# Inverse of the gated delta rule: X and its transpose on different partition halves, products over four quarters of the TensorE array, Z and X in two PSUM banks

## What is computed

```python
mem = DECAY * mem + sdt
hard = (mem > THR).astype(x.dtype)
...
alpha = jax.nn.sigmoid(abt + alpha_spike * spike)
beta = jax.nn.sigmoid(bbt[..., None] + jnp.sum(spike * beta_spike, axis=-1, keepdims=True))
active = (jnp.sum(hard, axis=-1, keepdims=True) > 0)
alpha = jnp.where(active > 0, alpha, jnp.ones_like(alpha))
beta = beta * active
s = s * alpha[..., None]
u = jnp.einsum('bhd,bhdv->bhv', kt, s)
s = s - beta[..., None] * jnp.einsum('bhd,bhv->bhdv', kt, u)
s = s + beta[..., None] * jnp.einsum('bhd,bhv->bhdv', kt, vt)
out = jnp.einsum('bhdv,bhd->bhv', s, qt)
```

## Time and profile before

| | us |
|---|---|
| median of the 3 timed runs | 1183.43 |
| lowest and highest of them | 1169.3, 1190.45 |
| the profiled execution | 1186.2 |
| its span | 1184.5 |
| PE busy, PEld busy | 1079.8, 769.0 |
| DVE busy, ACT busy | 701.1, 519.5 |

### The profile page before, as it was taken

One profiled execution on the slowest core, in us unless ns is written; L12 is line 12 of the kernel. 1 busy time (PEld: TensorE's weight loads), 2 busy tenths in 40 slices (PEclk: granted clock), 3 DMA queues, 4 the chain that ended last, 5 costly groups with the idle time before them and its releaser, 6 DMA issues. The chain is left out here.

```text
span 1184.5 us, 41088 instructions
## 1 busy us (share of the span) xinstructions
PE 1079.8 (91%) x17266; PEld 769.0 (65%) x17266; DVE 701.1 (59%) x2517; ACT 519.5 (44%) x1500; POOL 200.7 (17%) x390
## 2 busy tenths in 40 slices
PE   7878789999999999999999997898999999899987
PEld 3332278888888888888888884456456456545642
DVE  2887868888878888887776551244336225323610
ACT  7566213444444444444444343144254245325411
POOL 7100101122122122212211201211103001110200
PEclk8999759999999999999999898899999999899999
DMA  2000000000000000000000003100000000000000
GB/s 89 1 1 1 1 2 3 5 4 4 4 4 4 4 5 4 4 4 4 4 27 4 4 4 101 31 1 1 0 9 10 1 9 1 10 1 1 10 1 9
DMA packets 12805, 11.38 MB, mean 10 GB/s; under 512 B 1563, under 2 KB 11407, under 8 KB 12623
## 3 DMA queue, kind: packets, MB, share of 16 engines
q1 hardware_dynamic: 12623, 8.75, 2.5%
HBM read 7.70 MB, written 1.05 MB: 7 GB/s over the span
## 5 line engine op out<-in xcount | busy, mean ns | idle before, releaser
L1220 ACT COPY work<-banks 128x128 f32<-128x128 f32 x160 | 42.8, 268 | 168.8 <-PE banks L926 168.8
L892 PE MATMUL banks<-work 64*64 64x64 f32 x3072 | 102.6, 232 | 6.7 <-DVE gates L599 5.8
L926 PE MATMUL banks<-work,gates 64*64 64x32 f32 x2560 | 105.3, 221 | 3.1 <-issue 2.8
L946 PE MATMUL banks<-work 64*64 64x32 f32 x2560 | 105.5, 223 | 0.4 <-ACT work L1220 0.4
L203 DVE SCALAR_TENSOR_TENSOR mom<-gates 128x16 f32<-128x16 f32 x512 | 101.3, 198 | 5.8
L926 PEld LDWEIGHTS banks<-work,gates 64*64 64x64 f32 x2560 | 93.5, 139 | 15.4 <-issue 11.4
L599 DVE COPY_PREDICATED gates<-work,banks 128x256 f32<-128x256 uint32 x192 | 101.9, 531 | 1.1
L199 DVE SCALAR_TENSOR_TENSOR gates<-mom,gates 128x16 f32<-128x16 f32 x512 | 96.7, 189 | 9.6 <-ACT gates L1193 4.5
L604 DVE TENSOR_TENSOR work<-work,banks 128x128 f32<-128x128 f32 x128 | 36.8, 288 | 101.1 <-PE banks L936 99.9
L936 PEld LDWEIGHTS banks<-work 64*64 64x64 f32 x2048 | 74.2, 139 | 32.9 <-issue 22.3
L946 PEld LDWEIGHTS banks<-work 64*64 64x64 f32 x2560 | 92.2, 139 | 0.5 <-ACT work L1220 0.5
(11 more groups left out here) (235 smaller groups left out, 2348.9 us busy)
## 6 DMA issues: line engine op xcount, KB each, us to landing
qT<-in_x_dram SPq DMA_DIRECT2D x4, 256.0 KB, 4.3
work<-in_x_dram SPq DMA_DIRECT2D x4, 256.0 KB, 4.0
out_dram<-work SPq DMA_DIRECT2D x4, 256.0 KB, 3.1
gates<-in_w_ff_dram SPq DMA_DIRECT2D x3, 256.0 KB, 3.1
wv_sb<-in_wv_dram SPq DMA_DIRECT2D x1, 512.0 KB, 4.9
work<-in_w_out_dram SPq DMA_DIRECT2D x1, 512.0 KB, 5.3
gates<-in_x_Wq_dram SPq DMA_DIRECT2D x1, 512.0 KB, 5.9
gates<-in_x_Wk_dram SPq DMA_DIRECT2D x1, 512.0 KB, 6.6
```

Source lines behind the costliest of these rows:

```text
L892: last = pe.matmul(level_out(l)[to, a], KS[rows, n.two, hp], late[rows, hp], start=True, stop=True)
L926: last = pe.matmul(packed(psZX, l)[rows, hp], EA[rows, n.three, l, hp], first_half(X, l)[rows, hp], start=True, stop=True)
L946: last = pe.matmul(packed(psXT, l)[rows, hp], Z[rows, l - 1, hp], second_half(XT[:, n.two], l)[rows, hp], start=True, stop=True)
L1220: ac.copy(first_half(Z[:, l - 1], l), packed(psZX, l)).then_inc(z_ok, 1)
```

## The change

Slots and halves of the heads are dealt anew, so that `make_z`, `make_x`, `turn_start` and `solve` go round four quarters (`by_time`), with the outputs of the two input halves in different banks: `psZX` is now banks 6 and 7. `make_xt` (`straight`) and `read_chunk` (`halves`) stay on two quarters. XT's output moves to the second half of bank 5, where the spike counts were; the counts go to unused columns of bank 0 (for gates above number 4), by a matmul of their own, `spike_counts`. Orders and waits follow from the shared banks: `spike_sums` moves from the end of l = 3 to between `make_x` and `make_xt` of l = 4, `spike_counts` stands behind that `make_xt`, `drive` moves forward in l = 4, `alpha` moves behind `keep(aft2, 0)`. `start_xt` (ACT) is three copies in place of one. `level` and `make_xt` get waits on the gates.

```diff
-        psZX, psXT = bank[6], bank[7]
+        psZX = paired(6)
+        psZX_half = psZX[:, :, 0:W]
+        psXT = psG[:, B * C:B * C + HP * W].rearrange("p (a n) -> p a n", a=HP)
...
+        def counts(g):
+            if g.n <= HP:
+                return psG[:, B * C:2 * B * C]
+            return psL[:, 0:2, 2 * C:4 * C]
...
+        by_time = [(par, 2 * t + (t + swap) % 2) for par in range(2) for swap in range(2) for t in range(2)]
+        by_parity = [(par, 2 * t + (par + swap) % 2) for t in range(2) for swap in range(2) for par in range(2)]
+        halves = [(par, 2 * t + s) for par in range(2) for s in range(2) for t in range(2)]
+        straight = [(par, 2 * t + s) for par in range(2) for t in range(2) for s in range(2)]
...
+        def at_level(par, hp):
+            return head_rows[hp // 2], 2 * par + (hp // 2 + hp) % 2
+
+        def at_x(par, hp):
+            return head_rows[hp // 2], 2 * (hp % 2) + par
+
+        def at_z(par, hp):
+            return head_rows[hp % 2], 2 * (hp // 2) + par
+
+        def at_xt(par, hp):
+            return head_rows[hp % 2], 2 * ((hp // 2 + hp) % 2) + par
...
                 def alpha(g):
                     ve.wait_ge(al0_ok, g.n + 1)
+                    ve.wait_ge(count_mm, g.n + 1)
...
+                        if l == 4 and gate:
+                            drive(gate)
                         spike(scan, h + 2)
                         if aft:
                             prefix(aft, l)
...
-                        if l == 4 and gate:
-                            drive(gate)
...
                         update(cur, 1)
-                    if gate:
-                        alpha(gate)
...
                         keep(aft2, 0)
+                    if gate:
+                        alpha(gate)
...
-                def level(n, l):
+                def level(n, l, gate=None, gate_old=None):
+                    if l == 1 and gate_old:
+                        pe.wait_ge(alpha_ok, gate_old.n + 1)
+                    if l == 3 and gate_old:
+                        pe.wait_ge(beta_ok, gate_old.n + 1)
...
-                    for hp in range(HP):
-                        for rows in head_rows:
-                            last = pe.matmul(packed(psZX, l)[rows, hp], XT[rows, n.two, hp],
-                                             first_half(Z[:, l - 1], l)[rows, hp], start=True, stop=True)
+                    for head in by_time:
+                        (rows, a), (_, z), (to, q) = at_xt(*head), at_z(*head), at_x(*head)
+                        last = pe.matmul(packed(psZX_half, l)[to, q], XT[rows, n.two, a],
+                                         first_half(Z[:, l - 1], l)[rows, z], start=True, stop=True)
...
-                def make_xt(n, l):
+                def make_xt(n, l, gate, gate_old):
+                    if l == 1 and gate_old:
+                        pe.wait_ge(be0_ok, gate_old.n + 1)
+                    if l == 5 and gate:
+                        pe.wait_ge(zal_ok, gate.n + 1)
...
+                def spike_counts(g, aft=None):
+                    if aft:
+                        pe.wait_ge(e_ok, aft.it * LEVELS + 4)
+                    if g.n:
+                        pe.wait_ge(beta_ok, g.n)
+                    pe.wait_ge(spk_ok, g.n + 1)
+                    pe.matmul(counts(g), bdones[:, :], counts_as(g, spk[:, g.two]), start=True, stop=True).then_inc(count_mm, 1)
...
-                    pe.matmul(psG[:, B * C:2 * B * C], bdones[:, :], spk[:, g.two], start=True, stop=True)\
...
                             make_x(nxt, l)
+                        if l == 4 and gate and gate.n <= HP:
+                            spike_counts(gate)
+                        if l == 4 and gate:
+                            spike_sums(gate)
                         if nxt:
-                            make_xt(nxt, l)
+                            make_xt(nxt, l, gate, gate_old)
+                        if l == 4 and gate and gate.n > HP:
+                            spike_counts(gate, aft)
                         if aft:
-                            level(aft, l)
+                            level(aft, l, gate, gate_old)
...
-                        if l == 3 and gate:
-                            spike_sums(gate)
...
-                    ac.copy(XT[:, n.two], EA[:, n.three, 0]).then_inc(x_init, 1)
+                    a = EA[:, n.three, 0].rearrange("p (r s) t -> p s r t", s=2)
+                    ac.copy(XT[:, n.two, 0:2], a[:, 0])
+                    for rows, other in (head_rows, head_rows[::-1]):
+                        last = ac.copy(XT[other, n.two, 2:4], a[rows, 1])
+                    last.then_inc(x_init, 1)
```

More of the change, by code:

```diff
@@ L923, in make_z @@
                         pe.wait_ge(x_ok, n.it * NX + l - 1)
-                    for hp in range(HP):
-                        for rows in head_rows:
-                            last = pe.matmul(packed(psZX, l)[rows, hp], EA[rows, n.three, l, hp], first_half(X, l)[rows, hp],
-                                             start=True, stop=True)
+                    for head in by_time:
+                        (rows, a), (_, q), (to, z) = at_level(*head), at_x(*head), at_z(*head)
+                        last = pe.matmul(packed(psZX_half, l)[to, z], EA[rows, n.three, l, a], first_half(X, l)[rows, q],
+                                         start=True, stop=True)
                     last.then_inc(z_mm, 1)
@@ L943, in make_xt @@
                         pe.wait_ge(xt_ok, n.it * NINV + l - 1)
-                    for hp in range(HP):
-                        for rows in head_rows:
-                            last = pe.matmul(packed(psXT, l)[rows, hp], Z[rows, l - 1, hp],
-                                             second_half(XT[:, n.two], l)[rows, hp], start=True, stop=True)
+                    for head in straight:
+                        (rows, a), (_, z) = at_xt(*head), at_z(*head)
+                        last = pe.matmul(packed(psXT, l)[rows, a], Z[rows, l - 1, z],
+                                         second_half(XT[:, n.two], l)[rows, a], start=True, stop=True)
                     last.then_inc(xt_mm, 1)
@@ L960, in correct @@
                     pe.wait_ge(kq_ok, (n.it + 1) * NKQ)
[L961 to L962 removed]
+                    for head in by_parity:
+                        (rows, hp), (to, a) = from_head(*head), at_res(*head)
                         last = pe.matmul(value_out[to, a], KQ[rows, n.four, 0, hp],
@@ L969, in solve @@
                     pe.wait_ge(xt_ok, (n.it + 1) * NINV)
-                    for hp in range(HP):
-                        for rows in head_rows:
-                            last = pe.matmul(value_out[rows, hp], XT[rows, n.two, hp], res[rows, hp, :],
-                                             start=True, stop=True)
+                    for head in by_time:
+                        (rows, a), (_, r), (to, q) = at_xt(*head), at_res(*head), at_x(*head)
+                        last = pe.matmul(value_out[to, q], XT[rows, n.two, a], res[rows, r, :],
+                                         start=True, stop=True)
                     last.then_inc(u_mm, 1)
@@ L1013, in read_chunk @@
                     pe.wait_ge(u_ok, n.it + 1)
-                    for hp in range(HP):
-                        for rows in head_rows:
-                            last = pe.matmul(o_out[rows, hp], EA[rows, n.three, LEVELS, hp], U[rows, hp, :],
-                                             start=False, stop=True, skip_group_check=True)
+                    for head in halves:
+                        (rows, o), (_, a), (_, q) = to_time(*head), at_level(*head), at_x(*head)
+                        last = pe.matmul(o_out[rows, o], EA[rows, n.three, LEVELS, a], U[rows, q, :],
+                                         start=False, stop=True, skip_group_check=True)
                     last.then_inc(o_mm, 1)
@@ L1102, in _ @@
                 project(8, 2)
+                spike_counts(first[0])
                 spike_sums(first[0])
@@ L1107, in _ @@
                 project(11, 2)
+                spike_counts(first[1])
                 spike_sums(first[1])
@@ L1113, in _ @@
                 project(14, 2)
+                spike_counts(first[2])
                 spike_sums(first[2])
@@ L1120, in _ @@
                 turn_z(3)
+                spike_counts(first[3])
                 spike_sums(first[3])
```

48 lines of the change are left out of this document (29 added, 19 removed).

## The result

The kernel after took 1250.11 us (1243.21 to 1251.5) against 1178.28 for the kernel before: a ratio of 1.0625, 95% interval [1.053, 1.072]. Ratios leave out executions in the chip's slower state, so they can differ a little from the quotient of two medians. The forecast was 1213, with a range to 1243. The sign was right, the size was not. The profiled execution has a span of 1249.8 us, 65.3 more than before, and a mean granted clock of 0.895.

A forecast was written before the change was run, and what follows sets the result against it. PE and DVE are both nearly full, so the order within one body was taken to bound the kernel. From a span of 1184.5, +17.2 for bodies and +12.3 for clock falls gave 1214.0, or 1213 on the median's footing; range 1178 to 1243.

The forecast's parts named there:

- The structure of a gated body: Level 0 to next level 0 in bodies with both gate jobs: +1.03 us, 18.27 a body, +24.7 for 24.
- the number of falls of the clock: Behind the new 2 us pause ahead of `beta_sums`, in 25 bodies: one in six, 4 falls, +12.3 us.
- The price of 3.07 a fall: `make_z(3)` to `make_z(4)` before: 7.02 us in body 25 at half speed against 3.95 in body 26.
- The new pauses are nearly twice as long: Reason against the rival without falls (1200.6 us, chance 0.25): new pauses against one of 1.26 that brought no fall.
- dense products follow each new pause: Reason for the rival without falls (1200.6 us, chance 0.25): full products stand right behind the pause ahead of `beta_sums`.
- The clock falls in about half the bodies: Rival: 12 falls behind the new pauses at 3.07 us, 36.8 in all, giving 1237 us; chance 0.12.
- falls in most bodies: Sign of being wrong: the granted clock falling in most bodies, where 4 falls were forecast.
- PE regains full speed within some 7 us: Reason against falls in half the bodies (chance 0.12), beside PE's work filling the pause at half clock.
- The bodies without gates: Six bodies of 15.29 us save at `level(2)`, l = 3 and l = 4: -1.3 each, -7.8 in all.
- `start_xt` as three copies costs nothing here: `level(4)` to next level 0: copies of at most 0.28 us each cost nothing, ACT being busy under half the time.
- Four quarters bring nothing at 32 columns: Rival: `make_z` and `make_x` stay at 0.55 us, 1238 with falls (1225 if only `make_x` stays slow); chance 0.10.
- The late `alpha` is absorbed: Rival: the 1.63 us ahead of `make_x(1)` falls away, body 0.60 shorter, 1160 us or 1145; chance 0.10.

The follow-up runs named there:

- Experiment 3: Kernel after with `alpha` at one of three earlier places in DVE's queue: behind `prefix` 1166.8 us, ahead of `diagonal` 1173.4, ahead of `keep` 1214.8.
- experiment 5: Kernel after with `beta_sums` freed from `alpha` (gates above 4), plus products reordered two in a row on one quarter: 1153.75 us, ratio 0.977.

## Why the prediction was wrong

**The structure of a gated body was right.** Body 1 after (the fence above) by the prediction's own steps, all in us:

| stretch | before | forecast | measured |
|---|---|---|---|
| level 0 to `beta_sums` | 1.23 | 2.86 | 2.91 |
| `beta_sums` to `make_x(1)` | 1.06 | 1.06 | 1.06 |
| to `make_x(2)` | 2.19 | 2.16 | 2.16 |
| to `make_x(3)` | 2.94 | 2.88 | 2.92 |
| to `correct` | 1.11 | 0.96 | 0.87 |
| to `turn_out` | 0.64 | 0.64 | 0.65 |
| to `make_z(4)` | 1.45 | 0.59 | 0.58 |
| to `make_x(4)` | 1.29 | 0.82 | 0.82 |
| to `level(4)` | 0.90 | 2.36 | 2.21 |
| to the next level 0 | 4.43 | 3.94 | 4.00 |
| body | 17.24 | 18.27 | 18.18 |

Only `level(4)` is off by more than 0.1. 24 such bodies are 22.3 us, forecast 24.7.

**The failed step is the number of falls of the clock.** The prediction said "I take one in six: 4 falls, +12.3"; there were 22 in the 24 bodies. The price of 3.07 a fall came from a two-quarter stretch and was too high (1.85 here), but 22 x 1.85 = 40.7 is 28 us more than 12.3. Its ground was two rows: a pause of 1.03 behind which the clock was low, and one of 1.26 behind which it wasn't. Experiment 3 shows what such rows are worth: around a pause of 1 us a fall is rare (2 in 24 at 0.77 and at 0.98, where one in six would be 4); but the new pause is 2.08. "The new pauses are nearly twice as long" stood in the text, and only moved a chance. That dense products follow each new pause, which I counted for the kernel, did not help: the clock is still full in `beta_sums` and `make_x(1)` (0.30, 0.32) and low in `make_xt(1)` (0.82).

**"The clock falls in about half the bodies", 0.12, was the nearest rival** and had the direction, and "falls in most bodies" was named as a sign of being wrong. Its reason against, "PE regains full speed within some 7 us", is true (6.8 us in most of the bodies) and protects nothing, because each body brings a new pause.

**The bodies without gates.** The step said -1.3 each, in six. Body 26 took 14.80 against 15.29: -0.5. From body 27 to the end of the rounds there were four falls, where before had two; together with the dense rest of the layer, 9.1 us were not given back, and how they divide is open. One term that failed is "`start_xt` as three copies costs nothing here": it leaned on ACT's busy share, where `keep_out` is queued behind the copies and PE waits for it. With the two exchanged the body takes 13.80, close to the forecast 14.0, but partly by luck, since `keep_out`'s place is only about half of what body 26 missed. From `make_z(4)` to its end the body after gained 0.12 of the 0.56 forecast; the other half is lost at its start, where `make_x(1)` comes 2.22 after level 0 instead of 1.51 (the kernel after, then before):

```profile
699.79 0.32 PEld L980 LDWEIGHTS banks<-work 64*64 64x64 f32 x16 [1.40 <-ACT work L1283]
...
635.07 0.54 PEld L936 LDWEIGHTS banks<-work 64*64 64x64 f32 x16 [0.47 <-ACT work L1220]
```

With the exchange that pause is still 1.14. What makes it is open.

The other two rivals are settled. *Four quarters bring nothing at 32 columns* is wrong: `make_z` and `make_x` take 0.32 to 0.36, `solve` 0.43. The Trainium skill, TensorE: Matmul & The Clock Gate, "The mechanism", ties the overlap of a weight load to another row group; `make_x` repeats its input half and takes 0.32 like `make_z`, and experiment 5 repeats whole quarters at 0.34 to 0.41, so the rule isn't what limits these products here. *The late `alpha` is absorbed* (1145 to 1160) didn't come true, since nothing absorbs it; but where `beta_sums` doesn't wait for it the kernel takes 1153.

The ledger: the forecast span was 1214.0, the measured one 1249.8. Falls in bodies 1 to 24 +28.4 (40.7 less the 12.3 forecast), bodies from 26 on +9.1, the structure of the gated bodies -2.4, start-up and body 25 +0.7: 35.8.

## What to carry to other kernels

In these kernels a repeated wait of TensorE, priced by the time that the engine stands, was priced too low. Ask whether the granted clock stays up, compare only with pauses of the same length, and where a trace has none, count the fall in every repetition as a main case. Look for what a moved instruction's waiter really needs (here a bank that `drive` had long read) before moving anything else. And a queue with a low busy share can still delay what stands behind a longer step in it, as ACT's did in body 26.

## What the runs showed of the hardware

- Pauses of TensorE of 0.77, 0.98, 1.54 and 2.08 us, once in a body of 17 to 18 us at the same place, went with a fall of the granted clock in 2, 2, 13 and 22 of 24 bodies, each in one profiled execution; the mean granted clocks over all four executions of each of these kernels (ten for 0.98) bear the order out, with 0.959 to 0.963, 0.952 to 0.963, 0.918 to 0.929 and 0.895 to 0.902. How much the pause weighs and how much the light groups ahead of it is open, since the place was never changed.
- A pause of 1.87 behind two-quarter products brought it down in 24 of 24, for 10 to 17 us instead of mostly 6.8.
- Three identity products of 512 columns in the pause kept the clock up in bodies 1 to 25 of both kernels: 29 us gained in the one, 112 in the other.
- At 1.2 GHz 16 loads with 32 columns take 0.93 us on two quarters and 0.52 on four, at 2.4 GHz 0.54 and 0.32.
